# The experts' second product with gelu's output stationary and the weights moving

## The reference, cut to what matters

```python
def _L0_ffn_ref(x, Wg, bg, W1, b1, W2, b2):      # D, E, H, K = 64, 8, 128, 2
    gate_scores = x @ Wg + bg
    _, idx = jax.lax.top_k(gate_scores, K)
    mask = jax.nn.one_hot(idx, E, dtype=x.dtype).sum(axis=-2)
    xf, mf = x.reshape(-1, Dv), mask.reshape(-1, E)
    h = jax.nn.gelu(jnp.einsum('td,edh->teh', xf, W1) + b1[None], approximate=False)
    y = jnp.einsum('teh,ehd->ted', h, W2) + b2[None]
    out = jnp.einsum('ted,te->td', y, mf)
# and around it:
    h = h + _L0_ffn_ref(_layernorm(h, axis=-1), ...)
```

## Time and profile before

| | us |
|---|---|
| median of 3 runs | 3946.29 (3943.28 to 3951.18) |
| the profiled execution | 3942.37 |
| its span, first to last instruction | 3940.6 |
| TensorE matmul busy | 3751.8 (95%) |
| VectorE busy | 3135.7 (80%) |
| ScalarE busy | 2391.8 (61%) |
| first to last step of the decoder | 2166.2 to 3902.7 |

### The profile page before, as it was taken

The page is one execution under the profiler, slowest core; times in us unless marked ns, Lnnn a source line. Parts: engine busy times, 40 slices in busy tenths (PEclk is TensorE's granted clock), DMA queues, the critical chain, the costliest instruction groups (busy, mean ns, idle before and its releaser), DMA issues. The chain is left out here.

```text
span 3940.6 us, 159991 instructions
## 1 busy us (share of the span) xinstructions
PE 3751.8 (95%) x61932; PEld 2744.1 (70%) x61932; DVE 3135.7 (80%) x21227; ACT 2391.8 (61%) x11882; POOL 85.2 (2%) x129
## 2 busy tenths in 40 slices
PE   6899899999999999999999899999999999999998
PEld 3233688888888888888888666666666666666664
DVE  5888899999999999999998677667776667776675
ACT  3223688888888888888888334444434444444443
POOL 6100000000000000000000000000000000000000
PEclk8999999999999999999999999999999999999999
DMA  3010000000000000000000000000000000000000
GB/s 90 18 26 20 8 3 3 3 3 3 3 3 3 3 3 3 3 3 3 3 3 5 4 8 8 6 6 8 8 8 6 8 6 8 8 8 6 6 8 7
DMA packets 49571, 34.01 MB, mean 9 GB/s; under 512 B 37661, under 2 KB 46877, under 8 KB 48806
## 3 DMA queue, kind: packets, MB, share of 16 engines
q1 hardware_dynamic: 48806, 23.77, 2.3%
HBM read 15.37 MB, written 8.39 MB: 6 GB/s over the span
## 5 line engine op out<-in xcount | busy, mean ns | idle before, releaser
L731 PE MATMUL bank<-xs,ident 128*128 128x128 f16 x15583 | 1413.9, 222 | 0.0
L731 PEld LDWEIGHTS bank<-xs,ident 128*128 128x128 f16 x15583 | 1010.1, 102 | 252.3 <-issue 230.0
L751 ACT ACTIVATE ifg_cell_dec<-bank 128x48 f32<-128x48 f32 x1024 | 215.1, 210 | 640.4 <-PE bank L743 640.4
L743 PE MATMUL bank<-enc_lo,u_hi 128*128 128x16 f16 x8192 | 528.9, 173 | 0.3 <-DVE enc_lo L803 0.3
L740 PE MATMUL bank<-enc_hi,u_lo 128*128 128x16 f16 x8192 | 527.2, 172 | 0.0
L766 DVE SCALAR_TENSOR_TENSOR terms_dec<-ifg_cell_dec 128x32 f32<-128x32 f32 x1024 | 196.7, 192 | 397.9 <-ACT ifg_cell_dec L751 386.7
L740 PE MATMUL bank<-enc_hi,u_hi 128*128 128x16 f16 x8192 | 500.5, 169 | 0.0
L740 PEld LDWEIGHTS bank<-enc_hi,u_lo 128*128 128x128 f16 x8192 | 338.8, 96 | 206.4 <-DVE enc_hi L797 171.9
L758 ACT ACTIVATE bank<-twice_cell_dec 128x16 f32<-128x16 f32 x1024 | 191.7, 187 | 402.2 <-DVE twice_cell_dec L772 402.2
L743 PEld LDWEIGHTS bank<-enc_lo,u_hi 128*128 128x128 f16 x8192 | 338.6, 96 | 67.8 <-DVE enc_lo L803 0.4
L740 PE MATMUL bank<-ring_hi,u_lo 128*128 128x16 f16 x4096 | 260.4, 172 | 102.0 <-DVE ring_hi L797 95.5
(11 more groups left out here) (268 smaller groups left out, 7889.5 us busy)
## 6 DMA issues: line engine op xcount, KB each, us to landing
g_rows<-tok_d_gamma_batched_dram SPq DMA_DIRECT2D x8, 512.0 KB, 6.5
x_rows<-in_x_dram SPq DMA_DIRECT2D x16, 256.0 KB, 3.1
kept_h<-tok_ln_h SPq DMA_DIRECT2D x32, 128.0 KB, 2.1
res<-kept_h SPq DMA_DIRECT2D x32, 128.0 KB
out_dram<-sums SPq DMA_DIRECT2D x32, 128.0 KB
raw_wd<-in_L_attn_Wd_dram SPq DMA_DIRECT2D x2, 256.0 KB
raw_experts<-in_L_ffn_W_dram SPq DMA_DIRECT2D x2, 256.0 KB
raw_u<-in_L_attn_Uf_dram SPq DMA_DIRECT2D x1, 256.0 KB
```

Of the source, the lines that this page charges most:

```text
L731: nc.tensor.matmul(spare, m.ident16[:], m.xs[:, 0, :, :].rearrange("p b t -> p (b t)"), start=False, stop=True, skip_group_check=True)
L743: last = nc.tensor.matmul(z[k], m.u_hi[c.d][:, g, :], h_lo, start=False, stop=True, skip_group_check=True)
L751: nc.scalar.activation(c.ifg_cell[:, 0:3, :], ifg, ACT.Tanh, scale=1.0 / Z_SCALE).then_inc(c.s_t_ifg, 1)
```

## The change

The second product swaps its sides. Stationary is now a block of 128 tokens of `hid`, moving are the expert's 64 columns of `w2`, both float32 as before. One product of 512 columns becomes four of 64 columns with four weight loads of 128 columns, which are eight passes in place of two. `y_bank` then has tokens in rows and 256 columns in use. So ScalarE's copy (piece 36), the four transposes (pieces 37 and 38), the tile `ff_yT` and their two semaphores go. The bias becomes twelve products of 64 columns, all in piece 33. VectorE's addition stays in piece 43 and reads `y_bank`. The wait for the previous tile's addition moves from the first product of expert 0 (piece 14) to its second one (piece 19). And `idle_products` has new numbers: body steps 0, 1, 2, 19 and 20 go from 0, 4, 5, 5, 9 to 6, 6, 9, 7, 12, and the even steps 22 to 30 from 4 to 9. Steps 3 to 18 and the odd ones keep theirs.

```diff
-    by_place = {0: 0, 1: 4, 2: 5, 19: 5, 20: 9}
-    return by_place.get(step, 4 if step % 2 == 0 else 6 if step % STEPS == STEPS - 1 else 5)
+    by_place = {0: 6, 1: 6, 2: 9, 19: 7, 20: 12}
+    return by_place.get(step, 9 if step % 2 == 0 else 6 if step % STEPS == STEPS - 1 else 5)
...
-                    if e < 2:
-                        if e == 0 and past_first(j):
-                            pe.wait_ge(s_sum, j)
-                    else:
+                    if e >= 2 or past_first(j):
                         pe.wait_ge(s_hid, E * j + e - 1)
...
+                def expert_out(j, e, blocks):
+
+                    for blk in blocks:
+                        last = mm(y_bank[:, blk * D:(blk + 1) * D], hid[:, e % 2, blk * P:(blk + 1) * P], m.w2[:, e, :],
+                                  start=(e == 0 and blk == 0), stop=False, skip_group_check=True)
+                    if e == E - 1:
+                        last.then_inc(s_y, 1)
...
-                    if s in (33, 35):
-
-                        for part in ((0, 1) if s == 33 else (2,)):
-                            last = mm(y_bank[0:D, :], m.b2[:, part, :], maskT[:], start=False, stop=(part == 2),
-                                      skip_group_check=True)
-                        if s == 35:
-                            last.then_inc(s_y, 1)
+                    if s == 33:
+
+                        for blk in range(QS):
+                            for part in range(3):
+                                mm(y_bank[:, blk * D:(blk + 1) * D], maskT[:, blk * P:(blk + 1) * P], m.b2[:, part, :],
+                                   start=False, stop=False, skip_group_check=True)
                     if s in (19, 20):
...
                         pe.wait_ge(s_hid, E * j + 1)
-                        cols = slice((s - 19) * HALF // 2, (s - 18) * HALF // 2)
-                        mm(y_bank[0:D, cols], m.w2[:, 0, :], hid[:, 0, cols], start=(s == 19), stop=False,
-                           skip_group_check=True)
+                        if s == 19 and past_first(j):
+                            pe.wait_ge(s_sum, j)
+                        expert_out(j, 0, range(2 * (s - 19), 2 * (s - 18)))
...
-                            mm(y_bank[0:D, :], m.w2[:, e, :], hid[:, e % 2, :], start=False, stop=False,
-                               skip_group_check=True)
+                            expert_out(j, e, range(QS))
...
-                    if s in (37, 38):
-
-                        if s == 37:
-                            pe.wait_ge(s_yT, j + 1)
-                        for blk in range(2 * (s - 37), 2 * (s - 37) + 2):
-                            last = mm(pre_bank[0][:, blk * D:(blk + 1) * D], yT[:, blk * P:(blk + 1) * P],
-                                      m.ident[0:D, 0:D], start=(blk == 0), stop=True, skip_group_check=True)
-                        if s == 38:
-                            last.then_inc(s_yt, 1)
...
-                    if s == 36:
-                        act.wait_ge(s_y, j + 1)
-                        S.copy(yT[:], y_bank[0:D, :]).then_inc(s_yT, 1)
...
-                        dve.wait_ge(s_yt, j + 1)
+                        dve.wait_ge(s_y, j + 1)
...
-                        TT(flat(sums), pre_bank[0][:, 0:QS * D], flat(h_kept), ALU.add).then_inc(s_sum, 1)
+                        TT(flat(sums), y_bank[:, 0:QS * D], flat(h_kept), ALU.add).then_inc(s_sum, 1)
```

More of the change, by code:

```diff
@@ L964, in decoder_and_experts @@
         hid = sb("hid", [HE, 2, HALF], F32)
-        yT = sb("ff_yT", [D, HALF], F32)
         s_own = sem("ff_dve_step")
         (s_res, s_proj, s_normed, s_high, s_h, s_hk, s_split, s_nT, s_xn, s_score, s_mask, s_mT, s_mk, s_pre, s_hid,
-         s_y, s_yT, s_yt, s_sum, s_out, s_rank) = (sem(n) for n in (
+         s_y, s_sum, s_out, s_rank) = (sem(n) for n in (
              "res_loaded", "projected", "normed_made", "normed_high_made", "ff_h_made", "ff_h_kept", "normed_split", "normed_turned",
              "xn_kept", "gate_scores", "mask_made", "mask_turned", "maskT_kept", "pre_made", "hid_made",
-             "ff_y_made", "yT_kept", "y_turned", "sum_made", "sum_stored", "rank_made"))
+             "ff_y_made", "sum_made", "sum_stored", "rank_made"))
         def tile_rows(tensor, j):
```

## The result

| | us |
|---|---|
| before, median of 6 runs | 3948.97 (3943.28 to 3953.99) |
| changed, median of 6 runs | 3960.53 (3959.7 to 3967.12) |
| ratio | 1.003, 95% interval 1.002 to 1.004 |
| profiled execution before / after | 3942.37 / 3959.7 (spans 3940.6 / 3957.9) |

The changed kernel is slower by 11.6 us or 0.3%. On a second chip it was 3956.47 against 3946.39, 1.0027 (1.0016 to 1.0037). The direction was right and the size was not: a term of 59 us was really 12, and a part of which I expected 2 us back cost 7 more.

A forecast was written before the change was run, and what follows sets the result against it. It took decoder step length, with TensorE's lateness behind `ring_hi`, and the end behind them as decisive. 58.6 - 1.6 - 5.9 - 2.0 = +49.1 us on a median of 3946.3 gave 3995 us, 1.2% slower; range for 8 in 10: 3978 to 4012.

The forecast's parts named there:

- What bounds the kernel: Decoder steps: a three-engine loop of 1.68 us; TensorE may come 0.33 us behind `ring_hi` free, even steps have 0.07 left.
- Part 1: Second product in eight passes: 0.11 us a pass, 1.03 to 1.04 in all, 0.03 to 0.04 more than before.
- Part 2: Decoder steps with more idle products: TensorE comes late, 0.25 us in each even step 22 to 30; 58.6 us more.
- Part 3: Body steps 5 to 7 without the transposes: 1.6 us less, and 5.9 less as ten falls to 1.2 GHz go.
- Part 4: End behind the last decoder step: last addition 2.2 us earlier, six experts 0.03 more each; 2.0 us gained.
- The rival on the clock: Decoder's new stretch: clock falls once in each body, 0.6 to 1.2 us each, 4013 to 4031 us; 10 in 100.
- The first rival: Even steps: passes faster or loads overlap more; at 0.08 a pass all idle products hide, 3937 us; 12 in 100.

The follow-up runs named there:

- half of the rows: Changed kernel with the second product on rows 0 to 63 of hid and w2 alone, leaving out half of each expert's hidden units: 4025.04 us, 1.0206 times before.
- full transposes: Kernel before, its four transposes put on 128 rows with rows 64 to 127 zeroed: 3935.84 against 3941.59 us, ratio 0.9985.
- old idle numbers: Changed kernel with the idle products' numbers of the kernel before, all else kept: 3938.92 us against 3941.59 for before, 0.9995.
- wide `w2`: Kernel before with w2 laid out twice side by side, making the second product's stationary side 128 by 128: 3939.5 against 3941.59 us, ratio 0.9996.

## Why the prediction was wrong

**What bounds the kernel**: right. The limit of 0.33 us behind `ring_hi` held: in the changed kernel the gates come 0.37 behind it (2754.36 to 2754.73) and the step is 0.04 long, on half of the rows 0.57 behind it and 0.25 long.

**Part 1, eight passes in 1.03 to 1.04: the step that failed.** Measured 0.92, with 0.08 less in front of them. The pace of 0.11 was exact (eight passes are busy 1.06 to 1.10 at 2.4 GHz in every kernel). What failed is the fixed charge around them, 0.20 us in all: I took 0.59 with entry and exit from the transposes and the wait of 0.19 in front as given. Both belong to the 64 by 128 and 128 by 64 shapes. The run on half of the rows put back 0.19 of it. The Trainium skill (TensorEngine Tiling (Array Packing), Key Properties) says that a change of tiling mode drains the engine. The traces agree in so far as plain products of 64 rows, 64 columns or 16 rows between full ones cost some 0.08 to 0.1 more at entry and as much at exit, and no load runs ahead there. I had weighed what the skill says of the cost of a load and not this.

**Part 2, +58.6 us**: right in form. Each full product behind the gates takes 0.20 off, so 0.25 becomes 0.04 and 0.31 becomes 0.11 for step 0, and step 19, which still follows the 16-row mask product and so gains the exit alone, goes from 0.12 to 0.02. 31 x (5 x 0.04 + 0.02) + 30 x (0.04 + 0.11) = 11 to 12 us. Less part 3's gains of 7.5 that leaves 4, and the decoder measured +4.3. Step 20 cost nothing, as forecast. The bias products went at 0.03 each.

**Part 3, -1.6 and -5.9**: right, both; body steps 5 to 7 are at 1.68, and no stretch at 1.2 GHz stands there. The full transposes show that it goes with their shape, which I did not say.

**Part 4, -2.0: wrong by 9.** The work is shorter as forecast, but I took the clock of before as given, and at 1.2 GHz the end measured +6.9. The rival on the clock named the place wrongly: not the decoder, where idle products stand, but the end, where none do.

**The first rival** had its point of decision in a pass of 0.08. It came near by another road: at a pace of 0.11 the product was 0.20 cheaper than my sum, where 0.25 would have hidden all idle products. Even so the end's +6.9 would have eaten the other gains, as the run with the old idle numbers shows (0.9995).

## What to carry to other kernels

Read a product's price with its neighbours: the shape of the stationary side decides whether the next load hides, so take the duration from a product that uses the same rows and columns of the array, and try to pad a 64-column or 64-row stationary side to 128 if full products stand around it. It shows in the time only where TensorE is late or its clock falls: the wide `w2` alone gained nothing that can be told. Work that only fills a wait has to be counted again whenever what stands beside it changes, here by 0.056 us a piece against a margin of 0.07. And where a stretch has few and small products, its clock in the old kernel is not the clock of the new one; look at what brought it up.

## What the runs showed of the hardware that was not expected

- Between full products, a float32 product of 64 rows costs more than one of 128: 1.03 us against 0.92 for eight passes with exit, and 0.19 against 0.11 in front.
- A load of 128 float32 columns hides under the 512 moving columns of another pass (the full old product took 0.95 in all). So does one of 64 columns within the 128 by 64 product (its two loads in 0.19 us), and yet that product took 1.00: what shows is the load at the change of shape, not a load's length. The Trainium skill (TensorE: Matmul & The Clock Gate, The mechanism) says in one line that loads overlap running matmuls only where the row groups differ, and in another that they may also go to a background buffer. The trace disagrees with the first: the loads of the full products, all on the same rows, start up to 0.11 ahead of their matmuls.
- Where TensorE was at 1.2 GHz, as in the changed kernel's last 38 us, the new form's loop of experts did not get the clock back up in any of four profiled kernels; started at 2.4 GHz, the same loop kept it for 15 us in each profile of the four kernels with idle products in front of it (two of these have further ones in the loop).
